# One block for the whole front: GpSimd takes the block scales and the normalisation, and the first projections move into the feed-forward loop

## The chip, the cores and the metric

One core of a Trainium2 chip runs the kernel. The metric is the device time of one execution in microseconds (us), the median of several runs. PE is TensorE, DVE is VectorE, ACT is ScalarE, GpSimd is also called POOL, and SP issues most DMAs (SPq in the rows).

## What is computed

Two transformer layers over 8 sequences of 512 tokens with 128 features. Both layers add an attention and an FFN to x, and both read the layer-normed x. Layer 0 (the part the change touches):

```
xn = layernorm(x)                       # per token, 128 features
x  = x + attention0(xn) + ffn0(xn)

# attention0: c = xn W_DKV (128->32); k = c W_UK; v = c W_UV; q = xn W_UQ; causal softmax, 16 heads of 8; W_O
# ffn0: every linear is fp4_linear(x, w) = quant(x) @ quant(w).T
h  = silu(fp4_linear(xn, w_gate)) * fp4_linear(xn, w_up)    # 128 -> 352
y  = fp4_linear(h, w_down)                                  # 352 -> 128

# quant: per block of 16 values, scale = max(max|v| / 6, 1e-12);
# v / scale is rounded to {0, .5, 1, 1.5, 2, 3, 4, 6} with its sign, and multiplied by scale again
```

Layer 1 has 16-head attention with biases and a distance penalty `alpha * |i - j|`, and a top-2-of-32 expert FFN. The changed code prepares only its constants: alpha, its bias rows `qrows`, and the row numbers and tables for routing.

## The kernel before

**Stages.** `program` (L1569) runs `load_constants` (L233), `layernorm_stats` (L408), `ffn` (L518) with `prepare_ffn_weights` (L451) in it, `prepare_values` (L744) and `attention` (L760). Each has its own block: at the end of one, all engines meet before the next begins. Buffers of a finished block are given to later ones.

`load_constants`: SP loads alpha (three small transfers), the identity and x in four parts (L298), then waits for the DVE's alpha rows, stores them (L300), and only then loads the FFN's weights (L307, L309) and the tables. GpSimd issues five constants (L321). The DVE computes softplus of alpha with two ACT functions (L340 to L350), the alpha rows (L351 to L355), and sets the query tile Q to zero (L358). `layernorm_stats`: 32 batch statistics in a hardware loop (L422), mean and reciprocal deviation. `prepare_ffn_weights`: the DVE quantises all three weight matrices as one tile of 1120 columns; PE transposes them, ACT copies them out.

**Quantising** is in two helpers of eight DVE steps. `quant_scales` (L371): largest magnitude per block (L373), scale (L375), reciprocal (L377). `quant_grid` (L380): multiply by the reciprocal (L384), mask out the exponent (L386), turn it into a rounding constant with max and multiply (L388), add it (L390) and subtract it (L392). A ninth step multiplies by the scale (L579 in the FFN, L483 for the weights).

**The FFN loop.** `run_ffn_steps` (L501) writes the same software pipeline for each engine: iteration `it` runs from -2 to 8, and stage `(off, f)` does `f(it + off)` where such a sequence exists; the middle four iterations are a hardware loop of two rounds. The order of each engine is that of its list:

```
DVE: [(0, sh), (1, sm), (0, sh_rest), (1, sm_rest), (2, sx), (-1, s10)]
ACT: [(-1, a10), (1, a5), (2, a1_rest)]
PE:  [(-1, p10), (1, p5), (2, p1)]
```

`sx` normalises four tiles (L588) and quantises xn whole. `sh` quantises h (1408 columns) up to the grid, `sh_rest` multiplies by its scales. `sm` and `sm_rest` form two tiles each of h = silu(gate) * up (L606, one input in PSUM). `s10` adds the FFN's output to x (L618). `p1` transposes xn (L670), `p5` transposes quantised x (L678) and does gate and up (L684, L685) for four tiles in two PSUM buffers, so tile i waits until the DVE has formed h of tile i - 2. `p10` transposes quantised h in three chunks through one PSUM bank (L695), each copied out by ACT (`a10`, L650), then does 24 matmul instructions (L704). ACT also copies xn and quantised x (L629, L635) and does the silu (L642). SP loads the attention weights (20 transfers), fills the slot table (24 transfers, L553) and stores transposed xn of each sequence in DRAM (L558). GpSimd only loads the constant rows of K (L657).

**Then** `prepare_values` sets the value tile V on the DVE (L751, L756). The attention's order is written out by `script(k)` (L135), a list per step of half a sequence's heads. Step 0 begins with the entries `PJ` (projections of sequence 0): SP reloads transposed xn (L898); PE computes the latent vector (L1046), Q (L1048) and K (L1050); ACT copies each as float and bfloat16 (L1201, L1212, L1213); GpSimd splits each in three bfloat16 parts (`split`, L1520); SP writes twelve copies of parts to DRAM (`write_first`, L913, L917) and loads them as stacks into Q and K (`load_stack`, L919, L922). The first score matmul (L1135) needs the stacks of half 0. Later sequences' projections (`PN`) run inside the steps.

## Time and profile before

| | |
|---|---|
| median of 3 runs | 1447.19 us (1446.47 to 1448.09) |
| the profiled execution's own time | 1455.56 us |
| its span, first to last instruction | 1453.5 us |
| busy share of the span | PE 85%, DVE 64%, ACT 45%, GpSimd 20% |
| mean granted TensorE clock | 0.913 |
| first score matmul of the attention | 263.3 us after the span's start |
| from there to the end | 1190 us |

A timeline row gives start, busy length, engine, line of the kernel, operation and tiles, count where equal ones are merged, and in brackets how long the engine idled before it and what ended that. A window row gives the length of the stretch, each engine's busy time in it, the mean granted TensorE clock (1.00 is 2.4 GHz, 0.50 is 1.2 GHz), the DMA engines' busy share, and GB/s.

### The profile page before, as it was taken

Reading aid. Unit: us, or ns where it says so; the run is one execution under the profiler, and the core shown is the slowest. Engines: PE = TensorE matmul, PEld = TensorE weight load, DVE = VectorE, ACT = ScalarE, POOL = GpSimd, SP = SyncE. Lnnn points to the kernel's source line nnn. Section 1 sums busy time; section 2 is a strip of 40 time slices with the busy share of each in tenths; the row PEclk is TensorE's granted clock in tenths of the full one; section 3 lists DMA queues with packets and bytes.
Section 4 is the critical chain, followed back from the end, with each engine's and each line's share of the span. In section 5 each row is a group of like instructions: output and inputs, shape, how many; then the busy total and the mean of one; then the engine's idle time right before and its main releaser. Section 6 shows DMA issues by size and latency. Waiting matters only on the chain.

```text
span 1453.5 us, 25444 instructions
## 1 busy us (share of the span) xinstructions
PE 1230.2 (85%) x9691; PEld 718.1 (49%) x9691; DVE 928.4 (64%) x1586; ACT 652.4 (45%) x1245; POOL 295.8 (20%) x282
## 2 busy tenths in 40 slices
PE   0467763598999999998899999999988999999987
PEld 0245551244555555554454545555555655555543
DVE  6689991556787787888868655464543653554523
ACT  1122221135565556553454444455454455544554
POOL 0000001212211121022020443431222322231220
PEclk9877775679999999998999999899999998999999
DMA  3610001435323432442322242244533442441133
GB/s 100 177 57 8 14 8 55 79 64 103 83 60 68 103 77 45 88 99 46 76 53 40 41 103 47 63 80 113 121 90 77 122 93 58 114 101 50 32 101 92
DMA packets 115739, 109.01 MB, mean 75 GB/s; under 512 B 13986, under 2 KB 108324, under 8 KB 115236
## 3 DMA queue, kind: packets, MB, share of 16 engines
q1 hardware_dynamic: 108180, 95.83, 29.4%
q0 software_dynamic: 7440, 11.58, 3.0%
q8 instruction: 76, 1.25, 0.4%
q14 instruction: 43, 0.35, 0.1%
HBM read 65.25 MB, written 48.71 MB: 78 GB/s over the span
## 4 chain that ended last, share of the span: by engine, by line
PE 61%; DVE 11%; ACT 5%; issue 3%; DMA 2%; SPq 1%; POOL 0%; ACTq 0%; DVEq 0%
PE a_psO L1169 13%; PE a_psA L1135 11%; PE a_psB L1153 11%; PE a_psB L1027 6%; DVE a_maxes L1390 5%; PE a_psA L1027 3%; PE a_psM L1118 2%; PE a_psM L1113 2%; ACT a_Pt L1236 2%; ACT slots_flat L1259 2%; PE a_psA L1025 1%; PE a_psM L1187 1%; PE a_psB L1025 1%; PE a_psM L1048 1%; DMA K<-a_stack 1%
## 5 line engine op out<-in xcount | busy, mean ns | idle before, releaser
L1390 DVE TENSOR_REDUCE a_maxes<-a_psA 128x2 f32<-128x1024 f32 (+3 forms) x432 | 508.5, 1181 | 266.2 <-PE a_psA L1027 147.0
L1236 ACT ACTIVATE a_Pt<-a_psB 128x512 f32<-128x512 f32 (+1 forms) x864 | 460.4, 580 | 414.3 <-PE a_psB L1027 266.9
L1153 PE MATMUL a_psB<-Q,K 75*128 75x512 bf16 (+3 forms) x1024 | 328.8, 351 | 26.2 <-ACT a_Pt L1236 22.6
L1135 PE MATMUL a_psA<-K,Q 72*128 72x512 bf16 (+3 forms) x1024 | 317.0, 356 | 35.4 <-DMA K<-a_stack 20.5
L1169 PE MATMUL a_psO<-a_Pt,V 128*32 128x512 f32 (+3 forms) x2048 | 240.1, 549 | 8.7 <-ACT a_Pt L1236 8.7
L1135 PEld LDWEIGHTS a_psA<-K,Q 72*128 72x128 bf16 x1024 | 102.6, 101 | 152.4 <-issue 54.4
L1027 PE MATMUL a_psB<-dist,alpha_eye 128*128 128x128 bf16 x1536 | 175.2, 223 | 0.0
L1027 PEld LDWEIGHTS a_psB<-dist,alpha_eye 128*128 128x128 bf16 x1536 | 133.3, 100 | 66.0 <-issue 7.7
L1522 POOL TENSOR_TENSOR a_qkf<-a_qkf,a_parts 128x512 f32<-128x512 f32 x32 | 37.0, 1157 | 570.3 <-ACT a_parts L1213 570.3
L1027 PE MATMUL a_psA<-dist,alpha_eye 128*128 128x128 bf16 x1024 | 143.4, 221 | 0.0
L1153 PEld LDWEIGHTS a_psB<-Q,K 75*128 75x128 bf16 x1024 | 101.0, 99 | 83.5 <-ACT a_Pt L1236 53.9
L1027 PEld LDWEIGHTS a_psA<-dist,alpha_eye 128*128 128x128 bf16 x1024 | 101.8, 99 | 69.9 <-issue 8.9
L1516 POOL DMA_INDIRECT y<-a_spare,r_sent_id x64 | 61.3, 958 | 222.7 <-DVE a_spare L1455 149.2
L1025 PE MATMUL a_psA<-mask_q,identb 128*128 128x128 bf16 x512 | 102.2, 231 | 0.0
L1025 PE MATMUL a_psB<-mask_k,identb 128*128 128x128 bf16 x512 | 97.7, 222 | 0.0
L1503 POOL DMA_INDIRECT xs<-slots_flat,slots x64 | 62.0, 968 | 123.6 <-DVE a_maxes L1390 115.6
L1169 PEld LDWEIGHTS a_psO<-a_Pt,V 128*32 128x32 f32 x2048 | 42.3, 109 | 46.5 <-issue 16.8
L1025 PEld LDWEIGHTS a_psA<-mask_q,identb 128*128 128x128 bf16 x512 | 53.0, 103 | 3.4 <-issue 3.0
L1025 PEld LDWEIGHTS a_psB<-mask_k,identb 128*128 128x128 bf16 x512 | 51.0, 100 | 0.0
L1462 DVE COPY V<-a_psM 128x128 f32<-128x128 f32 x64 | 14.1, 282 | 56.3 <-PE a_psM L1062 50.1
L704 PE MATMUL f_ps_d<-wdT,f_hqT 128*128 128x128 f32 (+1 forms) x192 | 41.6, 411 | 7.4 <-DVE x L618 5.3
L704 PEld LDWEIGHTS f_ps_d<-wdT,f_hqT 128*128 128x128 f32 (+1 forms) x192 | 39.7, 318 | 10.5 <-ACT f_hqT L650 10.5
(234 smaller groups left out, 1388.5 us busy)
## 6 DMA issues: line engine op xcount, KB each, us to landing
a_stack<-a_parts SPq DMA_DIRECT2D x192, 128.0 KB
slots_flat<-in_expert_w SPq DMA_DIRECT2D x96, 128.5 KB
Q<-a_stack SPq DMA_DIRECT2D x32, 384.0 KB
K<-a_stack SPq DMA_DIRECT2D x32, 384.0 KB
xs<-in_c_no_token SPq DMA_DIRECT2D x24, 258.0 KB, 6.1
slots_flat<-xs SPq DMA_DIRECT2D x24, 258.0 KB
a_xnT<-xnT_dram SPq DMA_DIRECT2D x16, 256.0 KB
slots_flat<-y SPq DMA_DIRECT2D x16, 256.0 KB, 4.6
```

The lines of the kernel that those rows point to most:

```text
L704: m = pe.matmul(ps_d[:, i, :], hqT[0:r, q, i * P:(i + 1) * P], n.wdT[0:r, q, :], start=(q == 0), stop=(q == FFC - 1))
L1025: return pe.matmul(o, n.identb[:], mask[:], start=False, stop=True)
L1027: m = pe.matmul(o, n.alpha_eye[:, head, s, :], n.dist[:], start=False, stop=(s == parts_ - 1))
L1113: m = pe.matmul(psM[:, i * P:(i + 1) * P], ew[:, arg, i, 0:D], xT[:, arg, i * P:(i + 1) * P], start=True, stop=True)
L1135: pe.matmul(o, Q[0:A_ROWS, k % 4, h, i * P:(i + 1) * P], K[0:A_ROWS, k % 4, h, 0:w], start=True, stop=False)
L1153: pe.matmul(o, K[:, slot, h, kt * P:(kt + 1) * P], Q[:, slot, h, q0:T], start=True, stop=False)
L1169: m = pe.matmul(psO[32 * j:32 * (j + 1), q0:T], V[:, (k - 2) // 2 % 2, kt, r, j, :], Pt[:, (nB.at(k) + unit) % RING, x * w:(x + 1) * w], s ...
L1236: act.activation(Pt[:, u % RING, 0:w], psB[:, u % 2, 0:w], ACT.Exp).then_inc(p_ready, 1)
L1390: dve.tensor_reduce(maxes[:, k % 2, i, heads[0]:heads[0] + len(heads)], src, AX, ALU.max, negate=True).then_inc(a_free, 1)
L1503: pool.indirect_dma_start(out=n.xs_dram, out_offset=bass.IndirectOffsetOnAxis(ap=n.slots[:, j, t:t + 1], axis=0), in_=n.slots_flat[:, t * ...
L1516: pool.indirect_dma_start(out=n.y_dram, out_offset=bass.IndirectOffsetOnAxis(ap=sent_id[:, k % 2, e, i:i + 1], axis=0), in_=ys[e][:, i * D ...
L1522: pool.tensor_tensor(f, f, parts3[0], ALU.subtract).then_inc(split_step, 1)
```

## The change

`load_constants`, `layernorm_stats`, `prepare_ffn_weights`, `ffn` and `prepare_values` become one function, `first_layer_ffn`, with one block. Tiles and semaphores of the projections are allocated ahead of it. In it:

- SP loads alpha, then the FFN's weights, the identity, x (each quarter with its own semaphore), the attention weights, the tables and the slot table. It stores xn per sequence, and reloads that of sequences 0 and 1 in the last two of these. After the last it waits for the splits, writes the twelve copies, loads the stacks of halves 0 and 1, and stores the alpha rows last.
- The DVE computes alpha, quantises the weights, then does the statistics (no hardware loop). The alpha rows come in iteration 8.
- Quantising has seven steps: the scale is kept multiplied by 2^64, so that the mask and the OR of one constant give the rounding constant, and each of the two last steps applies a max to it as it adds or subtracts.
- GpSimd sets Q to zero and V to zero and ones, after its transfers. In the loop it normalises x (two passes over 512 columns) and multiplies by the scales of x and h.
- The lists are reordered: the gate products go ahead of `p10`, `s10` runs one iteration later and ahead of the h grid, and h is quantised in two parts (scales, then grid) with the first two products between them. All iterations are written out, with no hardware loop.
- The projections of sequence 0 run in iteration 6 on PE and ACT, their splits on GpSimd in iterations 6 and 7.

```diff
@@ quantising
-QUANT_STEPS = 8
-EXPONENT = 0x7F800000
-ROUND_HALVES = 1.5 * 2.0 ** 22
+QUANT_STEPS = 7
+UP = 2.0 ** 64
+OVER_TWO = 0x20800000
+HALVES_AT_TWO = 0x0B400000
+HALVES_UP = 1.5 * 2.0 ** -42
...
-    dve.tensor_scalar(unit.bitcast(I32), x.bitcast(I32), EXPONENT, None, ALU.bitwise_and).then_inc(sem, 1)
+    dve.tensor_scalar(unit.bitcast(I32), x.bitcast(I32), OVER_TWO, HALVES_AT_TWO, ALU.bitwise_and, ALU.bitwise_or
+                      ).then_inc(sem, 1)
     dve.wait_ge(sem, base + 5)
-    dve.tensor_scalar(unit, unit, 1.0, ROUND_HALVES, ALU.max, ALU.mult).then_inc(sem, 1)
+    dve.scalar_tensor_tensor(x, unit, HALVES_UP, x, ALU.max, ALU.add).then_inc(sem, 1)
     dve.wait_ge(sem, base + 6)
-    dve.tensor_tensor(x, x, unit, ALU.add).then_inc(sem, 1)
-    dve.wait_ge(sem, base + 7)
-    dve.tensor_tensor(x, x, unit, ALU.subtract).then_inc(sem, 1)
+    dve.scalar_tensor_tensor(x, unit, HALVES_UP, x, ALU.max, ALU.subtract).then_inc(sem, 1)
@@ SP, behind the loop's stores
+                for b in range(SEQS):
+                    sp.wait_ge(S["xn_kept"], b + 1)
+                    sp.dma_start(n.xnT_dram[b:b + 1].rearrange("o d t -> d (o t)"), xnT[:, b % 2, :]).then_inc(stored[b % 2], 16)
+                    if b >= SEQS - 2:
+                        sp.wait_ge(stored[b % 2], 16 * SEQS // 2)
+                        load_xnT(n, sp, b - (SEQS - 2))
+                sp.wait_ge(krows_loaded, 64)
+                sp.wait_ge(q_zeroed, 1)
+                for which in range(2):
+                    sp.wait_ge(n.parts_ready, which + 1)
+                    for r, part in enumerate((Q_PARTS, K_PARTS)[which]):
+                        sp.dma_start(n.scr[0, which, :, r * HD:(r + 1) * HD, :], n.parts[:, which, part, :]).then_inc(n.parts_written, 16)
+                sp.wait_ge(n.parts_written, 16 * 12)
+                load_stack(n, sp, 0)
+                load_stack(n, sp, 1)
+                sp.wait_ge(al_step, 14)
+                sp.dma_start(n.qrows.rearrange("h (r s) t -> (h r) s t", s=3), qb[:]).then_inc(al_stored, 16)
@@ DVE
-                run_ffn_steps(dve, [(0, sh), (1, sm), (0, sh_rest), (1, sm_rest), (2, sx), (-1, s10)])
+                def late(it, at):
+                    if it == SEQS and at == 0:
+                        alpha_rows()
+
+                run_ffn_steps([(0, sh), (1, sm), (-2, s10), (0, sh_rest), (1, sm_rest), (2, sx)], late)
@@ ACT
-                run_ffn_steps(act, [(-1, a10), (1, a5), (2, a1_rest)])
+                run_ffn_steps([(1, a5), (-1, a10), (2, a1_rest)], project)
@@ GpSimd
+                def nx(b, p):
+                    if b == 0:
+                        pool.wait_ge(bn_step, STATS)
+                    if b >= 2:
+                        pool.wait_ge(S["xn_turned"], b - 1)
+                        pool.wait_ge(S["x_grid"], QUANT_STEPS * (b - 1))
+                    tiles = slice(b * NT, (b + 1) * NT)
+                    xv = buf["xv"][:, p, :].rearrange("p (i d) -> p i d", d=D)
+                    pool.tensor_tensor(xv, n.x[:, tiles, :], bc(n.mean[:, tiles], D), ALU.subtract).then_inc(S["normed"], 1)
+                    pool.wait_ge(S["normed"], 2 * b + 1)
+                    pool.tensor_tensor(xv, xv, bc(n.rstd[:, tiles], D), ALU.mult).then_inc(S["normed"], 1)
+
+                def scale(w, b, p, turned):
+                    pool.wait_ge(S[w + "_grid"], QUANT_STEPS * (b + 1))
+                    if b >= 2:
+                        pool.wait_ge(S[w + "q_turned"], turned * (b - 1))
+                    pool.tensor_tensor(blocks(buf[w + "t"][:, p]), blocks(buf[w + "n"][:]),
+                                       bc(buf[w + "sc"][:], BLK), ALU.mult).then_inc(S[w + "_q"], 1)
...
+                pool.memset(n.Q[:].bitcast(F32), 0.0).then_inc(q_zeroed, 1)
+                pool.memset(n.V[:], 0.0).then_inc(v_zeroed, 1)
...
+                def split(it, at):
+                    s = {(SEQS - 2, 2): 0, (SEQS - 1, 1): 1}.get((it, at))
+                    if s is not None:
+                        pool.wait_ge(memsets, 1)
+                        pool.wait_ge(n.misc_free, s + 2)
+                        split_in_three(n, pool, n.qkf[:, s, :], [n.parts[:, s, x, :] for x in range(3)], 2 * s, n.parts_ready)
+
+                run_ffn_steps([(2, nx), (0, scale_h), (2, scale_x)], split)
@@ PE
+                def project(it, which):
+                    if it != SEQS - 2:
+                        return
+                    if which == 0:
+                        pe.wait_ge(S["xn_kept"], SEQS)
+                        pe.wait_ge(n.xnT_loaded[0], 16)
+                        pe.wait_ge(n.aw_loaded[0], 16 * 20)
+                        pe.matmul(ps_n[0:LATENT, :], n.aw[0]["dkv"][:], n.xnT[:, 0, :], start=True, stop=True).then_inc(n.misc_ready, 1)
+                        return
...
-                run_ffn_steps(pe, [(-1, p10), (1, p5), (2, p1)])
+                run_ffn_steps([(1, p5), (-1, p10), (2, p1)], project)
```

## Rows read from the trace of the kernel before

**Rows 1.** Windows: one cycle of the loop, part of the next, and behind the loop.

```profile
110.52:130.80 20.28, 14.62 (x60) 10.94 (x60) 19.00 (x28) 4.72 (x9) 0.00 (x0) 0.75 0.03 13
148.00:156.00 8.00, 6.30 (x29) 5.49 (x28) 7.76 (x10) 1.19 (x2) 0.00 (x0) 0.50 0.06 22
227.60:263.30 35.70, 6.06 (x6) 1.18 (x6) 3.85 (x11) 2.76 (x5) 7.08 (x6) 0.52 0.43 90
```

**Rows 2.** Timeline of the DVE ahead of the loop, and GpSimd's last transfers.

```profile
7.73 0.18 DVE L347 CAST al_parts_b<-alpha 128x17 bf16<-128x17 f32 x1
...
13.44 6.88 DVE L358 MEMSET Q<- 75x8192 f32 x1 [1.77 <-issue]
...
22.22 1.01 DVE L422 BATCH_NORM_STATS2 bn<-x  x4 [1.89 <-PEq L273]
...
34.11 1.32 DVE L373 TENSOR_REDUCE w_am<-w_raw 128x70 f32<-128x1120 f32 x1 [0.54 <-PEq L417]
...
46.55 1.12 DVE L588 TENSOR_SCALAR f_xv<-x,mean,rstd 128x128 f32<-128x128 f32 x4 [3.26 <-PEq L466]
47.05 2.82 POOL L657 DMA_DIRECT2D K<-in_c_krows  x4 [42.86 <-POOLq L466]
```

**Rows 3.** Timeline of the DVE in one cycle of the loop.

```profile
110.52 1.61 DVE L373 TENSOR_REDUCE f_ham<-f_hv 128x88 f32<-128x1408 f32 x1
...
113.14 1.62 DVE L384 TENSOR_TENSOR f_hn<-f_hv,f_hrs 128x1408 f32<-128x1408 f32 x1
...
115.72 0.89 DVE L388 TENSOR_SCALAR f_hu<-f_hu 128x1408 f32<-128x1408 f32 x1
...
118.31 1.62 DVE L392 TENSOR_TENSOR f_hn<-f_hn,f_hu 128x1408 f32<-128x1408 f32 x1
...
124.03 1.10 DVE L588 TENSOR_SCALAR f_xv<-x,mean,rstd 128x128 f32 x4
...
129.59 0.69 DVE L579 TENSOR_TENSOR f_xt<-f_xn,f_xsc 128x512 f32<-128x512 f32 x1
```

**Rows 4.** Timeline of the DVE and GpSimd where they overlap, in the attention.

```profile
279.55 3.49 DVE L1390 TENSOR_REDUCE a_maxes<-a_psA 128x4 f32<-128x1024 f32 x3 [0.87 <-PE a_psA L1025]
...
283.61 3.61 POOL L1562 TENSOR_TENSOR alpha_eye<-ident,alpha_parts 128x2048 bf16<-128x2048 f32 x1
...
283.73 3.54 DVE L1374 TENSOR_TENSOR a_maxes<-a_maxes,a_msplit 128x32 f32<-128x32 f32 x1
...
383.63 0.19 DVE L1374 TENSOR_TENSOR a_maxes<-a_maxes,a_msplit 128x32 f32<-128x32 f32 x1
```

**Rows 5.** Timeline of PE, ACT and DVE: gate products and p10, slow and fast.

```profile
54.02 0.60 ACT L635 ACTIVATE f_xqT<-f_ps_x 128x512 f32<-128x512 f32 x1 [4.55 <-PE f_ps_x L678]
...
59.66 0.53 DVE L606 TENSOR_TENSOR f_hv<-f_ps_u,f_silu 128x352 f32<-128x352 f32 x1 [1.22 <-ACT f_silu L642]
...
137.30 0.60 ACT L635 ACTIVATE f_xqT<-f_ps_x 128x512 f32<-128x512 f32 x1 [6.67 <-PE f_ps_x L678]
...
141.19 0.52 DVE L606 TENSOR_TENSOR f_hv<-f_ps_u,f_silu 128x352 f32<-128x352 f32 x1 [0.53 <-ACT f_silu L642]
...
204.34 0.66 PE L695 MATMUL f_ps_h<-ident,f_ht 128*128 128x128 f32 x4
...
208.36 4.57 PE L704 MATMUL f_ps_d<-wdT,f_hqT 128*128 128x128 f32 x24 [0.68 <-ACT f_hqT L650]
...
125.69 0.60 PE L695 MATMUL f_ps_h<-ident,f_ht 128*128 128x128 f32 x4
...
131.03 5.46 PE L704 MATMUL f_ps_d<-wdT,f_hqT 128*128 128x128 f32 x24 [1.03 <-DVE x L618]
```

**Rows 6.** Timeline from the loop's end to the first score matmul.

```profile
226.94 0.69 DVE L618 TENSOR_TENSOR x<-f_ps_d,x 128x512 f32<-128x512 f32 x1 [9.31 <-PE f_ps_d L704]
...
245.66 1.15 POOL L1522 TENSOR_TENSOR a_qkf<-a_qkf,a_parts 128x512 f32<-128x512 f32 x1
...
263.33 0.61 PE L1135 MATMUL a_psA<-K,Q 72*128 72x512 bf16 x1 [19.31 <-DMA K<-a_stack]
```

More of the change, by code:

```diff
@@ L366, with allocate_projections @@
-QUANT_STEPS = 8
-EXPONENT = 0x7F800000
-ROUND_HALVES = 1.5 * 2.0 ** 22
+def allocate_projections(n):
+    n.spare = n.sb("spare", [P, 2, T])
+    n.ckv = n.spare[0:LATENT]
+    n.xnT = n.sb("xnT", [P, 2, T])
+    n.qkf = n.sb("qkf", [P, 2, T])
+    n.parts = n.sb("parts", [P, 2, 3, T], BF16)
+    n.scr = n.dram("stack", (2, 2, HEADS, PRODUCT_ROWS, T), BF16)
+    n.misc_ready = n.sem("misc_ready")
+    n.misc_free = n.sem("misc_read")
+    n.split_step = n.sem("split_step")
+    n.parts_ready = n.sem("parts_ready")
+    n.parts_written = n.sem("parts_written")
+    n.xnT_loaded = [n.sem(f"xnT_loaded{p}") for p in range(2)]
+    n.stack_loaded = [n.sem(f"stack_loaded{s}") for s in range(4)]
@@ new lines, in load_xnT, with load_stack @@
+def load_xnT(n, sp, b):
+    src = n.xnT_dram if b < SEQS else n.xnT1_dram
+    sp.dma_start(n.xnT[:, b % 2, :], src[b % SEQS:b % SEQS + 1].rearrange("o d t -> d (o t)")).then_inc(n.xnT_loaded[b % 2], 16)
+def load_stack(n, sp, half):
+    t = half % 2
+    for s, dst in enumerate((n.Q, n.K)):
+        sp.dma_start(dst[0:PRODUCT_ROWS, half % 4],
+                     n.scr[half // 2 % 2, s, HALF * t:HALF * (t + 1)].rearrange("h r t -> r h t")
+                     ).then_inc(n.stack_loaded[half % 4], 16)
@@ L501, in run_ffn_steps @@
-def run_ffn_steps(engine, stages):
-    def iteration(it, shift):
-        for off, f in stages:
-            b = it + off
-            if 0 <= b < SEQS:
-                f(b + 2 * shift, b % 2)
-    for it in (-2, -1, 0, 1):
-        iteration(it, 0)
-    with engine.Fori(0, 2) as g:
-        for it in (2, 3):
-            iteration(it, g)
-    for it in range(6, SEQS + 1):
-        iteration(it, 0)
-def ffn(n):
-    nc = n.nc
-    HW = NT * FF
-    with ExitStack() as c:
-        prepare_ffn_weights(n, c)
+def run_ffn_steps(stages, between=None):
+    for it in range(-2, SEQS + 2):
+        for at, (off, f) in enumerate(stages):
+            if between is not None:
+                between(it, at)
+            if 0 <= it + off < SEQS:
+                f(it + off, (it + off) % 2)
@@ L632, in a5 @@
                     act.wait_ge(S["xq_turned"], b + 1)
-                    if not (isinstance(b, int) and b < 1):
+                    if b:
                         act.wait_ge(S["gate_up"], NT * b)
@@ L646, in a10 @@
                         act.wait_ge(S["hq_turned"], FFC * b + q + 1)
-                        if not (isinstance(b, int) and b < 1):
+                        if b:
                             act.wait_ge(S["down"], b)
@@ L665, in p1 @@
                 def p1(b, p):
[L666 to L667 removed]
+                    pe.wait_ge(S["normed"], 2 * b + 2)
+                    if b:
                         pe.wait_ge(S["xn_kept"], b)
@@ L674, in p5 @@
                     pe.wait_ge(S["x_q"], b + 1)
-                    if not (isinstance(b, int) and b < 1):
+                    if b:
                         pe.wait_ge(S["xq_kept"], b)
@@ L690, in p10 @@
                     for q in range(FFC):
-                        if q or not (isinstance(b, int) and b < 1):
+                        if q or b:
                             pe.wait_ge(S["hq_kept"], FFC * b + q)
@@ L698, in p10 @@
                     pe.wait_ge(S["hq_kept"], FFC * (b + 1))
-                    if not (isinstance(b, int) and b < 1):
+                    if b:
                         pe.wait_ge(S["added"], b)
@@ L741, in load_attention_weights @@
     return 16 * len(loads)
-def prepare_values(n):
-    n.V = n.sb("V", [P, 2, NT, 4, 4, 32])
-    zeroed, ones = n.sem("V_zeroed"), n.sem("V_ones")
-    with n.nc.Block() as block:
-        @block.vector
-        def _(dve):
-            dve.memset(n.V[:], 0.0).then_inc(zeroed, 1)
-            dve.wait_ge(zeroed, 1)
-            for r in range(4):
-                col = 16 * (1 - r // 2) + r % 2
-                for p in range(2):
-                    dve.memset(n.V[:, p, :, r, :, col], 1.0).then_inc(ones, 1)
-            dve.wait_ge(ones, 8)
 def attention(n):
```

503 lines of the change are left out of this document (217 added, 286 removed).

## The prediction

> **What bounds the kernel now.** I read the share of the span by windows first. The change rebuilds only what stands ahead of the attention's first score matmul, and that matmul starts at 263.3 us [rows 6]; the 1190 us behind it keep their code except for the projections of sequence 0, which leave step 0. So the question is when this matmul can start. Next the timeline of the DVE, stage by stage. Ahead of the feed-forward (FFN) loop everything is serial on the DVE: the memset of Q takes 6.88 us, statistics start at 22.22, the weights' quantisation at 34.11, the first normalisation at 46.55 after 3.26 us of idling at a block boundary [rows 2]. In the loop the DVE is busy 19.00 of a cycle of 20.28 us, PE 14.62, ACT 4.72, GpSimd not at all, at a mean granted clock of 0.75 [rows 1]: the DVE is the bound, but PE with its waits for ACT is close behind. The last addition ends at 227.6; then 35.7 us pass in which PE is busy 6.06 and the DVE 3.85 [rows 1, 6]: a memset, a load, three projections, two splits on GpSimd, twelve writes and the loads of Q and K, one behind another. Three places to gain, then: the head, the cycle, and the stretch behind the loop.
>
> **GpSimd beside the DVE: the price that decides.** GpSimd now normalises (2 passes of 128x512 per sequence) and multiplies by block scales (128x512 and 128x1408). While its 3.61 us pass over alpha_eye runs from 283.61, a DVE subtraction of 32 columns lasts 3.54 us and ends 0.05 after it; the same instruction takes 0.19 us later. Three reductions that overlap the GpSimd passes before it keep to 3.49 us, 1.16 each [rows 4]. So GpSimd's passes can shut out DVE passes with two SBUF inputs, while reductions from PSUM run on. The Trainium skill's page "SBUF — State Buffer", section "Who interferes with whom", says the second of the two to issue is blocked for a whole instruction where the DVE has two SBUF inputs or is in a 2-port mode; by that rule, which speaks against this change, the trace agrees.
>
> Passes of GpSimd: 1.15 us for 512 columns [rows 6]. For 1408 columns I scale that (3.2) and the 2048-column row (3.61 gives 2.5) [rows 4], and take 2.8.
>
> **The cycle.** Let 0 be the end of the DVE's x grid. From the DVE leave, per sequence: a one-input pass over 1408 (0.89), a scale pass over 1408 (about 1.62, as its equal in length), the normalisation (1.10), and the x forms of the first two (0.4, by the columns, and 0.69): 4.7 us [rows 3]. The two fused passes keep the length of the two-input ones. A bare subtraction from 20.3 gives 15.6, but the chain across engines is longer:
> - GpSimd scales x, 1.2; PE transposes, about 0.7 (1.1 at half clock); from ACT's copy to the end of the second h product 4.41 us with PE at full clock, 6.17 with PE slow [rows 5]. That is 6.3 or 8.5. The DVE has only the h scales to do meanwhile (2.62 [rows 3], delayed by at most one GpSimd pass), so it idles 2.5 to 5 us.
> - The addition, 0.69 [rows 6]: 7.0 or 9.2.
> - The h grid: from 113.14 to the end at 119.93, less the dropped pass (0.93 with its gap), 5.87 [rows 3]: 12.9 or 15.1.
> - The other two products, about 1.0: 13.9 or 16.1. GpSimd's h scaling runs until 15.7 or 17.9 and shuts out the small x scale step behind the reduction, which would start 0.7 on: 1.1 us lost.
> - The x part: from 125.1 (124.03 plus 1.10) to 130.28, less 0.4 and 0.7 for what leaves, 4.0 [rows 3]. Cycle 19.0 or 21.2.
>
> PE needs 8.6 us (204.34 to 212.9) or 10.8 us (125.69 to 136.5) for p10, of which 24 matmuls are 4.57 or 5.46 [rows 5], 7 for p5 and 0.7 for p1, 16.3 to 18.5: it fits, but again with some 2 us of idling in each cycle. The granted clock was 0.50 from 148 to 156 [rows 1], after such a pause; now the gate products come right behind the pause and would be the slow ones. I take the middle, 20.1 us. So the loop's steady state, which the 4.7 us were to shorten, gains next to nothing.
>
> **The head.** Alpha's casts come at 7.73 [rows 2]. GpSimd issues nine transfers, the last four in 2.82 us [rows 2], to about 7 us, and then sets Q and V. No row shows a GpSimd memset of any size. From below: the DVE's own rate, 6.88 for Q and, for half the elements, 3.4 for V; from above twice that. I take the lower end, since one output and no input is the cheapest pass there is. Whether it shuts out the DVE no row shows either; the nearest are [rows 4], where a GpSimd pass does so to the full, so I take that: the first cast waits until 13.9, the next until 17.3, alpha ends at 18.2. If not, alpha ends at 8.8. Both ends enter the range. Behind it: quantising the weights, 9.18 (34.11 to 3.26 ahead of 46.55) less 0.77 for one pass [rows 2], to 26.6; 32 statistics and their tail without loop branches, about 9.9 of the present 11.4, to 36.5 (x has landed long before); GpSimd's normalisation 2.3; x part 4.0; scaling 1.2; transposes 1.1. ACT's copy for sequence 0 comes at 45.1; before, at 54.02 [rows 5]: 8.9 earlier. The weights' transposes lie beside the statistics. On the SP queue the weights' seven transfers now go ahead of x; they are needed only at 18.2, so their order costs nothing under this cover. The first iteration then starts at 45.1 + 8.7 + 4.0 = 57.8 (the 8.7 us from that copy to the end of four products are as before), and the second at 78.8 with PE slow. Five cycles of 20.1 lead to iteration 6 at 179.3. Before, 110.52 + 4 x 20.3 = 191.7.
>
> **The tail.** From there PE is the bound: latent projection after the scale of x and ACT's copy (2.7), p5 (7.3), Q projection (1.3 to 2), p10 for sequence 5, K projection, p10 for 6 and 7 (8.6 to 10.8 each), last addition 0.7: 39 to 49, I take 44. The reordered s10 makes the DVE wait for sequence 5's p10 in iteration 7 and the h grid of 7 waits behind it, to about 28; GpSimd's K split, some 3.5 us, interleaves with that grid, so p10 for 7 finds its input at about 34, just when PE comes. Alpha rows (2.8 us) lie ahead of an addition that PE needs only 5 us into that p10. Beside it: K is split from about 24 on; from the start of that split to the score matmul it took 17.7 us before (245.66 to 263.33 [rows 6]), so 42 to 45. Both chains end together. Behind the addition about 1.5 us remain for a block boundary; V's memset, the xnT reload and the projections are gone from there. Score matmul at 179.3 + 44 + 1.5 = 224.8, against 263.3: 38.5 us saved. The tail alone costs 44 where it was 35.9 (191.7 to 227.6), and repays with the 35.7 behind it.
>
> The profiled execution took 1455.56 us for a span of 1453.5; the sum makes it 1417. The median of the runs stands 8.4 lower, at 1447.19, so the forecast is 1408.7, say **1409**.
>
> **Rivals.**
> 1. The memsets do not shut out the DVE (they read nothing). The weights start at about 9 and all is 9 us earlier: 1400. For it: no row shows the lock without a read. Against: the block in [rows 4] was complete, not in part. 0.27.
> 2. GpSimd is dearer: memsets at twice the DVE's time (+10.3) and 3.2 us for the h scaling (+2 over the loop): 1420. 0.15.
> 3. PE stays at full clock through the gate products and tail: cycle 19.0 (-5.5), tail 39 (-2, as the loads of K hold the start at about 42): 1401 with the memset lock, 1392 without. 0.10.
> 4. Slower: in the cycle no GpSimd pass finds a moment beside the DVE, so its 6.6 us lie on the chain with the DVE's 15.6 and the 5 us wait for the gate products at half clock: 27.2 us a cycle, 6 times 7.1 more, 43: 1451. It decides from a cycle of 26.5. Against: h scaling lies beside two PSUM products and a reduction, normalisation beside the wait for the gates. 0.03.
> That the change does not do what it says would need the K split or the stack loads to start only behind the loop; the waits are written otherwise.
>
> **How the numbers follow.** My own case holds 0.45, with 1401 to 1417 from the cycle's two ends. The range 1390 to 1428 takes in rivals 1 to 3 and leaves out the extremes of their sums. Within 0.2% (2.9 us, about what a measurement of this kernel tells from no change) or slower there is hardly anything: faster 0.96, same 0.01, slower 0.03.
>
> **What would show it.** Right: alpha's casts lengthened to several us beside a GpSimd memset; a cycle near 20 us with 2.5 us or more of DVE idle ahead of the first h product, ended by ACT; x's small scale step lengthened beside the h scaling; PE nearly without gaps from iteration 6; first score matmul near 225 us. Wrong: that matmul later than 245 or before 207, GpSimd passes in the loop above 4 us (then the DVE shuts out GpSimd and p10 starves), or a changed length of the attention behind it by over 4 us.

## The result, and the profile after

The changed kernel took 1409.62 us (median of 4 runs, 1409.07 to 1410.85) beside 1447.64 us for the kernel before on the same chip: ratio 0.972, 95% interval 0.967 to 0.977. Forecast were 1409.0, from 1390 to 1428. The profiled execution took 1409.59 us, its span 1407.7.

The windows of after, cut at the start of iterations 1 to 6, at the end of the last addition, and at the first score matmul:

```profile
77.33:97.95 20.62, 14.19 (x60) 9.65 (x60) 15.11 (x19) 4.81 (x9) 5.68 (x4) 0.78 0.04 14
97.95:117.71 19.76, 12.39 (x60) 8.46 (x60) 15.71 (x21) 4.80 (x9) 5.68 (x4) 0.90 0.04 14
117.71:138.05 20.34, 12.99 (x60) 8.88 (x60) 15.70 (x20) 4.81 (x9) 5.68 (x4) 0.84 0.04 14
138.05:158.47 20.42, 16.01 (x60) 11.74 (x60) 15.71 (x21) 4.56 (x9) 5.68 (x4) 0.68 0.00 0
158.47:178.49 20.02, 15.31 (x62) 10.34 (x62) 15.71 (x21) 5.05 (x10) 5.68 (x4) 0.83 0.10 32
178.49:220.90 42.41, 31.73 (x132) 24.28 (x132) 29.08 (x28) 10.35 (x19) 16.50 (x9) 0.72 0.33 74
220.90:226.70 5.80, 0.00 (x0) 0.02 (x1) 0.00 (x1) 0.00 (x0) 0.00 (x0) 0.68 0.85 149
226.70:1407.70 1181.00, 1093.44 (x9196) 625.61 (x9196) 741.67 (x1292) 603.38 (x1157) 282.88 (x263) 0.95 0.34 78
```

The DVE's busy time in a cycle fell from 19.00 us [rows 1] to 15.7, but the cycle only from 20.28 to 20.23 (mean of the five). The score matmul starts at 226.7 instead of 263.3 [rows 6], 36.6 us earlier. The head gives 12.9 of them: iteration 1 starts at 77.33, in the trace of before at 90.22. At the start of iteration 6 the lead is 13.4 (178.49 against 191.84). The tail from there to the end of the last addition takes 6.6 us more (42.4 against 35.8). The largest part, 29.9, comes from the stretch between the last addition and the score matmul: before, 35.7 us passed there [rows 1]; now 5.8, in which PE does nothing and the DMA engines are busy for 0.85 of the time. The attention behind takes 1181.0 us. Its 1190 in the profile of before belong to an execution 8.4 us above that kernel's median; if all of these 8.4 fell into the attention, which one trace cannot show, its length is unchanged.

The DVE's timeline of before, at the start of iteration 1, at the first h product of a later cycle, and at the start of iteration 6:

```profile
90.22 1.61 DVE L373 TENSOR_REDUCE f_ham<-f_hv 128x88 f32<-128x1408 f32 x1
...
119.85 0.52 DVE L606 TENSOR_TENSOR f_hv<-f_ps_u,f_silu 128x352 f32<-128x352 f32 x1
...
191.84 1.61 DVE L373 TENSOR_REDUCE f_ham<-f_hv 128x88 f32<-128x1408 f32 x1
```

The head, on the timelines of the DVE, GpSimd and ACT:

```profile
5.63 11.66 DVE L469 TENSOR_SCALAR al_e<-al_e 128x17 f32<-128x17 f32 x1 [0.36 <-ACT al_e L608]
...
6.81 7.00 POOL L655 MEMSET Q<- 75x8192 f32 x1
13.67 3.59 POOL L656 MEMSET V<- 128x4096 f32 x1
...
27.26 6.28 DVE L490 BATCH_NORM_STATS2 bn<-x 128x6 f32<-128x128 f32 x32
...
35.51 1.04 POOL L631 TENSOR_TENSOR f_xv<-x,mean 128x512 f32<-128x512 f32 x1 [17.78 <-DVE rstd L505]
...
43.97 0.60 ACT L581 ACTIVATE f_xqT<-f_ps_x 128x512 f32<-128x512 f32 x1 [4.50 <-PE f_ps_x L688]
```

A DVE instruction of 17 columns lasts 11.66 us, through both memsets. One cycle, and the end of the loop, on the timeline of all engines:

```profile
83.66 0.53 DVE L533 TENSOR_TENSOR f_hv<-f_ps_u,f_silu 128x352 f32<-128x352 f32 x1 [3.31 <-ACT f_silu L586]
...
92.38 2.59 POOL L639 TENSOR_TENSOR f_ht<-f_hn,f_hsc 128x1408 f32<-128x1408 f32 x1 [11.72 <-DVE f_hn L337]
...
93.80 1.21 DVE L318 TENSOR_SCALAR f_xsc<-f_xam 128x32 f32<-128x32 f32 x1
...
201.84 2.46 DVE L335 SCALAR_TENSOR_TENSOR f_hn<-f_hu,f_hn 128x1408 f32<-128x1408 f32 x1
...
202.89 2.53 POOL L302 TENSOR_TENSOR parts<-qkf,zeros 128x512 bf16<-128x512 f32 x1
...
215.32 0.47 SPq L448 DMA_DIRECT2D qrows<-al_rows  x1
...
220.21 0.69 DVE L545 TENSOR_TENSOR x<-f_ps_d,x 128x512 f32<-128x512 f32 x1 [6.65 <-PE f_ps_d L716]
...
226.71 0.58 PE L1121 MATMUL a_psA<-K,Q 72*128 72x512 bf16 x1 [6.53 <-PEq L410]
```

The DVE waits 3.31 us for the silu ahead of the first h product; in the same place of the loop before it did not wait at all (the row of 119.85, right behind the step of 118.31 in [rows 3]). The small x scale step takes 1.21 us beside GpSimd's h scaling and 0.18 alone. The score matmul is released by the end of the block, 11.4 us behind the issue of the alpha rows' store.

### The profile page after: what moved, and what is told of

Same layout as the page of the kernel before. It is cut to its first block, busy times and chain, and to the rows that moved or that the text cites. A ratio compares the mean times of both kernels' runs of the same rounds, so it can differ in the third digit from the quotient of the medians.

```text
span 1407.7 us, 25082 instructions
## 1 busy us (share of the span) xinstructions
PE 1217.6 (86%) x9691; PEld 712.3 (51%) x9691; DVE 903.2 (64%) x1511; ACT 651.4 (46%) x1245; POOL 355.2 (25%) x324
## 4 chain that ended last, share of the span: by engine, by line
PE 63%; DVE 11%; ACT 5%; issue 3%; DMA 1%; SPq 1%; POOL 0%; DVEq 0%; ACTq 0%
PE a_psO L1155 13%; PE a_psA L1121 11%; PE a_psB L1139 11%; PE a_psB L1011 6%; DVE a_maxes L1376 5%; PE a_psA L1011 3%; PE a_psM L1104 2%; PE a_psM L1099 2%; ACT a_Pt L1222 2%; ACT slots_flat L1245 2%; PE a_psA L1009 1%; PE a_psM L1173 1%; PE a_psB L1009 1%; PE a_psM L1175 1%; PE a_psM L1034 1%
## 5 line engine op out<-in xcount | busy, mean ns | idle before, releaser
L1376 DVE TENSOR_REDUCE a_maxes<-a_psA 128x2 f32<-128x1024 f32 (+3 forms) x432 | 508.5, 1181 | 233.3 <-PE a_psA L1011 164.7
L300 POOL TENSOR_TENSOR qkf<-qkf,parts 128x512 f32<-128x512 f32 x32 | 37.6, 1174 | 379.9 <-ACT parts L1199 377.8
L1502 POOL DMA_INDIRECT y<-spare,r_sent_id x64 | 61.3, 958 | 220.3 <-DVE spare L1441 147.6
L1502 POOL DMA_INDIRECT y<-r_before,r_sent_id x32 | 30.7, 960 | 49.6 <-DVE a_maxes L1376 44.1
L302 POOL TENSOR_TENSOR parts<-qkf,zeros 128x512 bf16<-128x512 f32 x32 | 41.8, 1306 | 2.5
```

The lines of the kernel that those rows point to most:

```text
L300: pool.tensor_tensor(f, f, parts3[0], ALU.subtract).then_inc(n.split_step, 1)
L302: pool.tensor_tensor(parts3[1], f, n.zeros[0:f.shape[0], :], ALU.add).then_inc(n.split_step, 1)
L1376: dve.tensor_reduce(maxes[:, k % 2, i, heads[0]:heads[0] + len(heads)], src, AX, ALU.max, negate=True).then_inc(a_free, 1)
L1502: pool.indirect_dma_start(out=n.y_dram, out_offset=bass.IndirectOffsetOnAxis(ap=sent_id[:, k % 2, e, i:i + 1], axis=0), in_=ys[e][:, i * D ...
```

## The experiments

Each starts from the kernel after and changes one thing, where nothing else is said. The three groups of four ran on chips, or at times, that differ: the kernel before took 1462.65, 1449.49 and 1453.79 us in them. So times are compared within a group only, and the traces by stages. The stage columns are: end of the reciprocal deviation, mean cycle of iterations 1 to 5, time from iteration 6 to the last addition's end, from there to the score matmul, and that matmul's start (us).

| run | group | median | ratio to before, 95% | deviation | cycle | tail | gap | score matmul |
|---|---|---|---|---|---|---|---|---|
| e1_memsets_late | 1 | 1422.35 | 0.966 to 0.974 | 31.34 | 20.88 | 42.45 | 6.20 | 226.10 |
| e2_x_scale_dve | 1 | 1423.37 | 0.970 to 0.975 | 35.44 | 21.06 | 41.02 | 3.37 | 227.98 |
| e3_old_order | 1 | 1446.65 | 0.987 to 0.991 | 37.17 | 23.70 | 48.22 | 3.07 | 248.83 |
| e4_alpha_rows_early | 1 | 1420.39 | 0.968 to 0.973 | 37.19 | 20.39 | 41.99 | 0.62 | 223.13 |
| a0_after | 2 | 1412.67 | 0.968 to 0.979 | 35.42 | 20.87 | 40.22 | 8.77 | 230.57 |
| e5_x_part_first | 2 | 1391.71 | 0.955 to 0.967 | 37.18 | 17.28 | 39.26 | 2.27 | 205.76 |
| e6_head_spread | 2 | 1404.89 | 0.965 to 0.976 | 27.21 | 19.88 | 41.75 | 3.45 | 212.91 |
| e7_nx_held | 2 | 1407.71 | 0.966 to 0.977 | 35.43 | 20.49 | 41.02 | 1.42 | 222.07 |
| a1_after | 3 | 1414.46 | 0.969 to 0.977 | 37.16 | 20.23 | 42.43 | 5.93 | 228.57 |
| e8_store_first | 3 | 1410.61 | 0.965 to 0.973 | 35.42 | 20.87 | 42.46 | 1.09 | 224.97 |
| e9_all | 3 | 1383.91 | 0.945 to 0.955 | 27.06 | 17.28 | 38.11 | 0.62 | 193.16 |
| e10_all_x_scale_dve | 3 | 1381.82 | 0.946 to 0.954 | 26.98 | 17.21 | 36.72 | 0.99 | 190.66 |

### The kernel after again: a0 and a1

> The kernel after, unchanged, as the reference of this chip: on the chip of the first four experiments the kernel before took 1462.65 us, 1% more than the 1447.64 of the first comparison, and the attention behind the first score matmul 1195.8 to 1196.6 us instead of 1181.0. Theory (the chip is slower in the attention, the changed front is not): ratio to before again 0.972, cycles of 20.2 to 21 us, attention as long as in this call's other kernels within 2 us.

> The kernel after once more, as the reference of this call: earlier controls gave 1409.6 and 1412.7 us, the first score matmul at 226.7 and 230.6 us, 11.4 us behind the issue of the alpha rows' store both times. Expected: 1409 to 1424 by the chip, the same 11.4 us.

The ratio (0.974 and 0.973) and the 11.4 us behind the store (11.44 and 11.49) are as expected. The front's stages repeat, but in two forms each. The deviation comes near 35.4 (the first profile, a0) or near 37.2 (a1, where the lock caught an earlier instruction, see the last section). The loop takes 20.23 us a cycle (the first profile and a1) or 20.87 (a0, and e1 and e8 with the same loop). In the slower form the second h product of iteration 2 comes 2.34 us behind the first, in the faster 1.34. The granted clock tells the two apart. Take iterations 1 to 5 of these five traces, 25 cycles. Where the clock between the two products was 0.98 to 1.00, they lie 1.34 to 1.54 us apart; where it was 0.50 to 0.51, 2.34 to 2.35; where it rose in between (0.59 to 0.77), 1.95 to 2.35.

The attention took 1184.1 us in a0 and 1184.6 in a1, but 1194.6 to 1196.6 in group 1, on unchanged code. Within group 2 it was expected to agree within 2 us and did not: 1183.1 to 1189.6. For the kernel before, the median of each group less the 265.4 us ahead of and around the attention in its one trace (263.3, and 2.1 outside the span) gives an estimate of 1197, 1184 and 1188 us; the changed kernels' traces show 1195 to 1197, 1183 to 1190 and 1185 to 1189. So nothing speaks for a changed attention, and why its length varies stays open.

### The head: e1 and e6

```diff
+                pool.wait_ge(w_quantised, 1)
                 pool.memset(n.Q[:].bitcast(F32), 0.0).then_inc(q_zeroed, 1)
```

> Only change against the kernel after: GpSimd starts the memsets of Q and V when the weights are quantised, not right behind its transfers. Theory (a GpSimd memset shuts the DVE out, 11.66 us in one instruction): the instruction at 5.63 us lasts 0.2 us, alpha ends near 8, the weights are quantised from about 8.5 to 17 instead of 18.95 to 27.3. The statistics then meet x, whose last quarter lands near 28, and their small steps with two inputs meet the late memsets (17 to 27.5): reciprocal deviation near 31 instead of 35.4, whole kernel 4 to 5 us faster than 1409.6, about 1405. Rival A (x is not late): 8.5 us faster, 1401. Rival B (the 11.66 us was no lock but a slow wait or ACT's second table load): the instruction stays long, nothing gained, 1409 to 1411.

The timeline of the DVE and GpSimd in e1:

```profile
5.85 0.38 DVE L469 TENSOR_SCALAR al_e<-al_e 128x17 f32<-128x17 f32 x1 [0.36 <-ACT al_e L608]
...
11.80 1.32 DVE L316 TENSOR_REDUCE f_ham<-f_hv 128x70 f32<-128x1120 f32 x1 [3.15 <-DMA f_hv<-in_L_ffn_w_down]
...
20.25 6.92 POOL L656 MEMSET Q<- 75x8192 f32 x1 [13.37 <-DVE f_hn L559]
...
26.42 0.21 DVE L494 TENSOR_TENSOR mean<-bn 128x32 f32<-128x32 f32 x1
...
26.92 0.29 DVE L498 TENSOR_SCALAR mean<-mean 128x32 f32<-128x32 f32 x1
...
27.12 3.54 POOL L657 MEMSET V<- 128x4096 f32 x1
...
27.49 3.20 DVE L503 TENSOR_SCALAR bn_m<-bn_m 128x32 f32<-128x32 f32 x1
```

The 11.66 us become 0.38: the lock was real. The weights began at 11.8 and not at 8.5, held by their last transfer; the deviation came at 31.34, the "near 31" expected, but not for the reason expected: x held nothing, the weights' landing and V's memset did. The score matmul comes 4.5 us earlier than in a0, whose loop has the same length. The total cannot confirm it: group 1 has no run of the kernel after, and against the kernel before the ratios are 0.970 here and 0.972 for after, with intervals that overlap. The rows also tell which instructions a memset shuts out: a TENSOR_SCALAR of 32 columns beside V's lasts 3.20 us, a TENSOR_TENSOR with two SBUF inputs beside Q's 0.21. The Trainium skill's page "SBUF — State Buffer", section "Who interferes with whom", says just this: a two-input DVE instruction contends with GpSimd's reads, not with one that only writes, while a TENSOR_SCALAR may be in a 2-port mode, which contends. The trace agrees on both, though no run shows in which mode the blocked TENSOR_SCALAR was.

```diff
+                pool.wait_ge(al_step, 9)
+                pool.memset(n.V[:], 0.0).then_inc(v_zeroed, 1)
                 for s in range(4):
                     pool.dma_start(n.K[PRODUCT_ROWS:ROWS, s],
...
+                pool.wait_ge(w_quantised, 1)
                 pool.memset(n.Q[:].bitcast(F32), 0.0).then_inc(q_zeroed, 1)
-                pool.memset(n.V[:], 0.0).then_inc(v_zeroed, 1)
```

> GpSimd sets V when alpha is done (near 8.5 us), then issues the four transfers of K's constant rows, and sets Q when the weights are quantised; the rest as after. In e1 the weights' quantisation began at 11.8 (its last transfer landed then, beside K's rows), and V's memset held the statistics' tail for 3.0 us. Theory (what is left of the head there is the landing of the weights beside K's rows, and V's memset): weights from 9.5 to 10.5 on, done near 18, Q's memset hidden beside the 6.3 us of statistics, reciprocal deviation near 27 instead of 35.4, first iteration 8 us earlier than a0. Rival (the 2 MB of x behind the weights bound it): statistics wait for x until 20 or later and the deviation is there near 30 to 31, 4 to 5 us earlier than a0, as in e1.

The timeline of the DVE and GpSimd in e6:

```profile
8.68 3.51 POOL L652 MEMSET V<- 128x4096 f32 x1 [4.49 <-DVE alpha_parts L477]
8.78 1.32 DVE L316 TENSOR_REDUCE f_ham<-f_hv 128x70 f32<-128x1120 f32 x1 [0.15 <-DMA f_hv<-in_L_ffn_w_down]
10.13 2.11 DVE L318 TENSOR_SCALAR f_hsc<-f_ham 128x70 f32<-128x70 f32 x1
...
19.00 6.28 DVE L490 BATCH_NORM_STATS2 bn<-x 128x6 f32<-128x128 f32 x32
19.14 6.92 POOL L658 MEMSET Q<- 75x8192 f32 x1 [3.91 <-DVE f_hn L559]
```

Without K's rows beside them the weights land 3 us earlier than in e1, and the statistics keep their 6.28 us beside Q's memset. The deviation comes 8.2 us earlier than in a0: the theory holds, and x bounded nothing. The median is 7.8 us lower, but that it is so near 8.2 is chance: in the traces the score matmul comes 17.7 us earlier (8.9 by iteration 1, 5.0 in five shorter cycles, 5.3 in the gap, less 1.5 in the tail), and the attention takes 5.5 longer.

### The cycle: e3, e2, e7, e5

```diff
-                run_ffn_steps([(1, p5), (-1, p10), (2, p1)], project)
+                run_ffn_steps([(-1, p10), (1, p5), (2, p1)], project)
...
-                run_ffn_steps([(1, a5), (-1, a10), (2, a1_rest)], project)
+                run_ffn_steps([(-1, a10), (1, a5), (2, a1_rest)], project)
...
-                run_ffn_steps([(0, sh), (1, sm), (-2, s10), (0, sh_rest), (1, sm_rest), (2, sx)], late)
+                run_ffn_steps([(-2, s10), (0, sh), (1, sm), (0, sh_rest), (1, sm_rest), (2, sx)], late)
```

> PE and ACT go back to the order of before (p10 and a10 ahead of the gate products); the addition s10 goes first on the DVE, since p10 waits for it; the rest as after. Theory (chain): the gate products start only behind p10, whose 8.6 us (10.8 at half clock) from the iteration's start plus 6.5 us for the products come ahead of the h grid's rest, so a cycle is x_q 1.2 + p10 8.6 to 10.8 + gate to second product 4.4 to 6.2 overlapped in part: 22.5 to 24 us, DVE idle 6 to 8 us in each; kernel 1424 to 1433. Rival (the order does not matter, PE is idle long enough in each cycle): cycle 20.2, kernel 1409 to 1411.

The timeline of the DVE in iteration 2 of e3:

```profile
102.75 1.61 DVE L316 TENSOR_REDUCE f_ham<-f_hv 128x88 f32<-128x1408 f32 x1
...
112.51 0.53 DVE L533 TENSOR_TENSOR f_hv<-f_ps_u,f_silu 128x352 f32<-128x352 f32 x1 [7.17 <-ACT f_silu L586]
```

The DVE idles 7.17 us and the cycle is 23.70, 2.8 over e1's, whose loop is that of after: inside the theory's 22.5 to 24. (Its absolute time was expected too low, by this group's slower attention.) The order of after (gate products first, the addition behind the first two h products) is thus worth 2.8 us a cycle, and 5.8 in the tail (48.22 against e1's 42.45). With the old order the kernel is 1.1% faster than before, not 2.8%: more than half of the gain hangs on this order.

```diff
+                    dve.wait_ge(S["x_grid"], QUANT_STEPS * (b + 1))
...
+                    dve.tensor_tensor(blocks(buf["xt"][:, p]), blocks(buf["xn"][:]), bc(buf["xsc"][:], BLK), ALU.mult
+                                      ).then_inc(S["x_q"], 1)
...
-                run_ffn_steps([(2, nx), (0, scale_h), (2, scale_x)], split)
+                run_ffn_steps([(2, nx), (0, scale_h)], split)
```

> The multiplication of quantised x by its block scales (128x512) goes back from GpSimd to the DVE, 0.69 us more on the DVE in each cycle; the rest as after. Theory (the cycle is a chain through x scale, p5, h products, h grid and x part, and the DVE idles 2.5 to 3.3 us in it): the 1.06 us on GpSimd with 0.16 us of hand-over become 0.69, the DVE's idle time ahead of the first h product falls to about 2.3, mean cycle 19.7 instead of 20.23, kernel about 1406.5. Rival (the DVE's work bounds the cycle): cycle 20.9, kernel 1414.

Neither came: 21.06 us a cycle against e1's 20.88. The wait ahead of the first h product did fall, to 2.60 us in every cycle, from 2.85 to 3.31 in e1. The timeline of the DVE and GpSimd in e2 says where that was lost again:

```profile
136.96 1.03 POOL L636 TENSOR_TENSOR f_xv<-x,mean 128x512 f32<-128x512 f32 x1
...
137.46 1.09 DVE L330 TENSOR_TENSOR f_xn<-f_xv,f_xrs 128x512 f32<-128x512 f32 x1
138.08 1.37 POOL L638 TENSOR_TENSOR f_xv<-f_xv,rstd 128x512 f32<-128x512 f32 x1
138.58 1.15 DVE L332 TENSOR_SCALAR f_xu<-f_xn 128x512 int32<-128x512 int32 x1
```

The x scale had been a gate: behind it the normalisation ran beside the wait for the gate products. Without it GpSimd goes on at once and lands on the x grid, where two steps take 1.12 us more (0.69 and 0.43 alone).

```diff
-                        pool.wait_ge(S["x_grid"], QUANT_STEPS * (b - 1))
+                        pool.wait_ge(S["x_grid"], QUANT_STEPS * b)
```

> As e2 (x scale on the DVE), but GpSimd's normalisation of sequence b waits until the x grid of sequence b - 1 is done, so it no longer runs beside that grid. In e2 two steps of the x grid took 1.09 and 1.15 us instead of 0.69 and 0.43 beside it, and its mean cycle was 21.1. Theory (the loss in e2 is that block, the chain itself is shorter): the x grid steps keep to 0.69 and 0.43, cycle 1.0 to 1.3 us under e2's, 0.3 to 0.5 under a0's. Rival (the DVE's added 0.69 us bounds it): cycle 0.5 to 0.7 over a0's.

With the normalisation held back (on top of e2) the two steps take 0.69 and 0.43 again and the cycle is 20.49, 0.38 under a0's 20.87, as the theory has it; under e2's it is 0.57, not the 1.0 to 1.3 expected. The 0.38 is partly the clock's: from the first h product to the second it is 2.15 us in e7's mean cycle and 2.30 in a0's. Against the faster form of after (20.23, with 1.74 between the products) e7 is 0.26 longer, and 0.15 shorter if that difference is taken out (an estimate). So one trace of each does not show that more work on the DVE makes the cycle shorter. It shows that a cycle with 0.6 us more DVE busy time (16.3 against 15.7) is not longer by that, as the rival wanted (0.5 to 0.7 over a0's): the DVE's work was not the bound, the chain was.

```diff
-                run_ffn_steps([(0, sh), (1, sm), (-2, s10), (0, sh_rest), (1, sm_rest), (2, sx)], late)
+                run_ffn_steps([(0, sh), (1, sm), (-2, s10), (2, sx), (0, sh_rest), (1, sm_rest)], late)
...
-                run_ffn_steps([(2, nx), (0, scale_h), (2, scale_x)], split)
+                run_ffn_steps([(2, nx), (2, scale_x), (0, scale_h)], split)
```

> The DVE's x part (scales and grid of x two sequences ahead) goes ahead of the h grid, and GpSimd scales x before h; the rest as after. Theory (the cycle is a chain: x grid, x scale on GpSimd, p5, first h products, h grid, x part): with the x part ahead of the h grid, p5 finds its input long before it needs it, and the DVE no longer waits for the gate products more than about 1 us; the cycle becomes the DVE's 15.7 us of work plus 1 to 2 us of blocked steps, 17.2 to 18.0, so 6 cycles save 14 to 18 us against a0 (20.2 to 20.8). Rival (PE with its waits for ACT, 16.3 us at full and 18.5 at half clock, bounds the cycle): 18.5 to 19, 8 to 10 us saved. Rival B (the h products of tiles 2 and 3 now end the DVE's iteration, and the next gate products wait for them): no gain.

The windows of two cycles of e5, and its timeline beside the x scale:

```profile
94.87:112.21 17.34, 12.70 (x62) 9.55 (x61) 15.06 (x19) 4.73 (x10) 7.00 (x5) 0.90 0.04 16
...
129.55:146.89 17.34, 11.36 (x64) 8.08 (x62) 15.06 (x19) 5.00 (x10) 7.00 (x5) 1.00 0.07 20
```

```profile
120.19 1.62 DVE L330 TENSOR_TENSOR f_hn<-f_hv,f_hrs 128x1408 f32<-128x1408 f32 x1
120.34 2.37 POOL L639 TENSOR_TENSOR f_xt<-f_xn,f_xsc 128x512 f32<-128x512 f32 x1 [6.12 <-DVE f_xn L337]
...
121.84 1.63 DVE L332 TENSOR_SCALAR f_hu<-f_hn 128x1408 int32<-128x1408 int32 x1
```

17.28 us a cycle and 21.0 us off the kernel: the chain through x is broken, since p5 now finds its input a whole part early. The total exceeds the 18 expected at most: the five cycles give 17.9, the tail is 1.0 us shorter too and the gap 6.5, while iteration 1 starts 0.6 later and the attention takes 2.1 longer. Neither rival came. (The splits keep their places on GpSimd: Q's behind the h scaling of sequence 6, K's ahead of that of 7.) Both windows last 17.34 us, at a granted clock of 0.90 and of 1.00, so the clock no longer sets the cycle here. The block works both ways: GpSimd, second to start, waits for L330 (2.37 us instead of 1.06), then L332 waits for GpSimd (1.63 instead of 0.89).

### The block's end: e4 and e8

```diff
-                    if it == SEQS and at == 0:
+                    if it == 2 and at == 1:
                         alpha_rows()
```
and the store of `qrows` goes from behind the stacks' loads to ahead of the twelve writes of parts.

> The five alpha-row steps go to iteration 2 of the loop, ahead of its first h product where the DVE idles 3 us, and SP stores the rows ahead of the twelve writes of parts. Theory (the block's end waits for the store of the alpha rows, issued at 215.3 and landed at 226.2 behind the stacks' loads): the gap between the last addition and the first score matmul falls from 5.8 to 2 to 3 us and the kernel to about 1406; iteration 2 is at most 1 us longer. Rival A (the stack loads, issued just ahead, end at the same time in any case): gap stays 5 to 6, kernel 1409 to 1411. Rival B (all five steps lie ahead of the last addition's path in the tail): a further 2 to 3 us, 1403.

The gap falls to 0.62 us, more than expected, and iteration 2 with the five steps takes 19.01 us, less than its neighbours (20.10 and 20.77), with the DVE busy for 18.46 of them and a granted clock of 1.00: the five steps lie where the DVE waited. The tail stays at 42: the rows did not lie on its path. e8 moves the store alone:

```diff
-                load_stack(n, sp, 0)
-                load_stack(n, sp, 1)
                 sp.wait_ge(al_step, 14)
                 sp.dma_start(n.qrows.rearrange("h (r s) t -> (h r) s t", s=3), qb[:]).then_inc(al_stored, 16)
+                load_stack(n, sp, 0)
+                load_stack(n, sp, 1)
```

> Only SP's order changes against after: the store of the alpha rows goes ahead of the four loads of the stacks, instead of behind them. In five traces the block ended 11.4 to 11.7 us behind that store's issue. Theory (the store lands last because 1.5 MB of stack loads are ahead of it, and the block's end waits for the store alone): it now lands 3 to 5 us behind its issue, long before the last addition; the gap from that addition to the first score matmul falls from 5.8 to 8.8 us to under 2, kernel 4 to 7 us faster than a1. Rival (the attention's first matmul then waits for the stacks of half 0, which land as late as the store did): gap 4 or more, under 2 us gained.

The timeline of e8 at the loop's end, and what the source view says of the store, first in after, then in e8:

```profile
216.44 0.33 SPq L446 DMA_DIRECT2D qrows<-al_rows  x1
...
223.19 0.69 DVE L545 TENSOR_TENSOR x<-f_ps_d,x 128x512 f32<-128x512 f32 x1 [6.58 <-PE f_ps_d L716]
224.97 0.39 PE L1121 MATMUL a_psA<-K,Q 72*128 72x512 bf16 x1 [1.82 <-DMA K<-stack]
```

```profile
DMA to landing us min/median/max: 10.9/10.9/10.9
```

```profile
DMA to landing us min/median/max: 2.9/2.9/2.9
```

The same 384 KB land 2.9 us behind their issue instead of 10.9. The gap is 1.09 us against 5.93 in a1, and the matmul's releaser is now the load of K. With the store last, a shorter tail only made the gap longer: tail and gap together are 49.0 us in a0 (40.22 and 8.77) and 48.4 in a1 (42.43 and 5.93), and 43.6 in e8. In the medians this shows as 3.9 us, with intervals that overlap; the traces carry the verdict.

### Together: e9 and e10

e9 is e5 and e6, with the alpha rows in iteration -1 ahead of `sm` and their store ahead of the parts. e10 has in addition e2's x scale on the DVE.

> Three edits together: the x part ahead of the h grid (e5), the head of e6, and the alpha rows' five steps in iteration -1, ahead of its first h product where the DVE idles 6.24 us, with their store ahead of the parts. Theory (the three lie in different stretches and add up): reciprocal deviation at 27.2 (35.4 in a1), mean cycle 17.3 (20.2 to 20.9), score matmul under 1.5 us behind the last addition, at 192 to 196 us instead of 227 to 230, kernel 32 to 36 us faster than a1. Rival (GpSimd or the loads of K's rows and x collide in the shorter head, or PE becomes the bound of the tail): 24 to 30 us.

> As e9, with the x scale (128x512) on the DVE instead of GpSimd. In e5 that GpSimd pass took 2.37 us instead of 1.06, and the DVE's pass L332 beside it 1.63 instead of 0.89: a block of 0.74 us in each cycle, as much as the 0.69 us that the pass costs on the DVE. Theory (a GpSimd pass beside two-port DVE passes gives back what it takes over): cycle 17.2 to 17.3, kernel within 1.5 us of e9. Rival (the DVE's work bounds the cycle and blocks cost nothing more): cycle 18.0, kernel 4 us slower than e9.

A window of one cycle, first of e9, then of e10:

```profile
102.42:119.75 17.33, 12.45 (x61) 9.40 (x60) 15.05 (x19) 4.70 (x9) 6.99 (x5) 0.90 0.04 16
```

```profile
100.95:118.28 17.33, 10.79 (x62) 7.77 (x60) 15.02 (x20) 4.70 (x9) 4.62 (x4) 1.00 0.04 16
```

And how each iteration of e10 starts, on its timeline:

```profile
118.28 1.62 DVE L316 TENSOR_REDUCE f_ham<-f_hv 128x88 f32<-128x1408 f32 x1 [1.91 <-POOL f_ht L644]
```

The edits add up: e9's score matmul comes 35.4 us earlier than a1's, and its median is 30.6 lower. The matmul falls within the theory's 192 to 196, the median just short of its 32 to 36; the attention behind was 3.6 us longer in its profile. e10's cycle is the same to 0.01 us: the DVE is busy for the same 15.0 us, once with 0.74 us of blocked time in it and once with 0.69 of work. What is left of the cycle can be read, too. In e5, e9 and e10 the DVE idles 1.9 us at the start of each full cycle, until GpSimd has multiplied h by its scales (2.59 us), since the next reduction waits until the scales that GpSimd reads may be written anew. No run takes this wait away. Both beat the kernel before and after; between them (0.9499 and 0.9503) nothing is told: the medians lie 2.1 us apart, where the theory allowed 1.5.

## Why the prediction was right, and where it was not

| step | forecast | measured |
|---|---|---|
| memsets of Q and V | 6.9, 3.4 | 7.00, 3.59 |
| weights start; end | 18.2; 26.6 | 18.95; 27.33 |
| statistics and tail | 9.9 | 8.2 |
| ACT's copy for sequence 0 | 45.1 | 43.97 |
| cycle | 20.1 (19.0 or 21.2) | 20.23; 20.87 in the other form |
| iteration 6 | 179.3 | 178.49 |
| tail | 44 | 42.41 |
| last addition to score matmul | 1.5 | 5.81 |
| score matmul | 224.8 | 226.71 |

- **The memset lock** was there, and e1 shows it by taking it away. Its form was another: not the casts waited, one behind each memset, but the one TENSOR_SCALAR before them waited through both memsets, and through the end of the transfers' issue. Alpha ended at 18.9, forecast 18.2 (8.6 in e1). What it cost the head is 4.1 us with the memsets alone moved (e1) and 8.2 with K's transfers moved too (e6). Rival 1 falls.
- **GpSimd's prices** (1.04 to 1.06 for 512 columns, 2.59 for 1408) were at or under those taken, so rival 2 falls.
- **The cycle** is the chain that the prediction summed: 3.3 us less busy time on the DVE than before (the 4.7 that leave, less some 1.4 of blocked steps: 1.0 in the x scale step, 0.4 in the h scale step) and no shorter cycle, DVE idle of 2.4 to 3.3 us ahead of the first h product, the x scale step lengthened by 1.0. That the order of work and not the amount is the bound is shown from three sides: the same work in another order takes 2.8 more (e3) or 3.6 less (e5), and more DVE work does not lengthen it by its amount (0.6 in e7; 2.8 in iteration 2 of e4, which was even shorter, at the full clock). Rivals 3 and 4 fall. The ends of 19.0 and 21.2 stood for PE at full and at half clock. The granted clock was 0.50 from 118 to 123 us of after, the stretch of the gate products, and 1.00 from 124 to 137; over 25 cycles the distance of the first two products goes with it. No run held the clock, so this is a correlation, a close one. What the whole move to GpSimd is worth was not measured: no run puts the normalisation or the h scaling back on the DVE, and none keeps the separate blocks.
- **The tail** came out at 42.41 us, with PE busy for 31.7. "PE nearly without gaps" holds only in so far as none of its twelve pauses there exceeds 1.3 us; together they are 10.0, most of them waits for ACT's copies, which the 8.6 to 10.8 us per p10 already contained. The K split interleaved with the h grid as forecast (2.46 us for a step of 1.62), but took 6.8 us instead of 3.5; PE waited 0.9 for the h scaling behind it. That the K chain and the last addition end together is seen in e8: its score matmul, released by the load of K, starts 43.6 us behind iteration 6, 1.1 behind the addition; forecast were 42 to 45.
- **The mis-sized term** is "Behind the addition about 1.5 us remain for a block boundary". It was 5.8: the block's end waits for the alpha rows' store, which SP issues behind 1.5 MB of stack loads and which lands 10.9 us later. e8 prices this at 4.8 us of the gap; 1.1 is left there, with K's load last, and 0.6 in e4 and e9, so 1.5 was enough for the boundary and the store was the step overlooked. It also means that in after neither PE's tail nor the K load ends the path, but SP's queue. It could have been read in the diff, where the store is SP's last transfer; its wait is the next line of the kernel.
- The errors offset each other: head -1.5 (iteration 1 at 77.3 for 78.8), cycles +0.7, tail -1.6, block end +4.3, sum +1.9 at the score matmul; the attention, forecast at 1181.8 from the median, took 1181.0. That the total came within 1 us of 1409 is partly luck. One sign of being wrong, an attention changed by over 4 us, is met by the letter (1190.2 and 1181.0 in the two profiles); the groups' medians, above, speak against a real change.

## What to carry to other kernels

Work taken off the busiest engine does not shorten a loop whose bound is a chain through several engines: follow one item round the loop first, and reorder so that its slowest leg starts a part earlier (3.6 us a cycle in e5). Give an idle GpSimd work only where the DVE reduces, reads PSUM or waits; elsewhere it can give back what it takes (0.74 us for 0.69 in e9 and e10). In a block's last transfers, put first what the block's end waits for, and last what only the next stage needs.
